# Node tiles of a graph transformer: distance between their starts, six slots where they are behind and ten elsewhere

## The chip, the cores and the metric

The kernel runs on one core of a Trainium2 chip. A core has a matrix engine (PE), a vector engine (DVE), a scalar engine (ACT), a general engine (POOL) that here only prepares gathers, and a queue engine (SP) that issues DMAs. The metric is the device time of one launch in microseconds (us); a lower time is better. The time before is the median of three runs, and beside it stands one execution that was recorded by the profiler.

## The reference

A graph of 6,250 nodes with 128 features and 200,000 edges, sorted by destination, goes through two layers of attention over edges and a feed-forward block; then comes a residual and a layer norm.

```python
for l in range(L):                                   # L = 2
    xn = _layernorm(x, ln1_g[l], ln1_b[l])
    deg = ...                                        # out-degree, normalised
    xp = xn + (xn @ Wpos[l] + bpos[l] + deg[:, None] * Wdeg[l][0] + bdeg[l])
    q, k, v = (xp @ Wq[l] + bq[l]), (xp @ Wk[l] + bk[l]), (xp @ Wv[l] + bv[l])   # 8 heads of 16
    att = jnp.einsum('ehd,ehd->eh', q[dst], k[src]) / scale       # one row per edge and self loop
    ex = jnp.exp(clip(att) - m[dst])
    alpha = ex / (s[dst] + 1e-16)
    aggr = segment_sum(v[src] * alpha, dst)
    x = x + (aggr @ Wo[l] + bo[l])
    h = gelu(_layernorm(x, ln2_g[l], ln2_b[l]) @ W1[l] + b1[l])
    x = x + (h @ W2[l] + b2[l])
return _layernorm(x0 + x)
```

## The kernel before

**The work.** Per layer there are edge units and node tiles. The edges lie in the order of their destination. 165 chunks of 1,024 edges each (`CA`) are gathered from the table of keys and values in memory: POOL issues eight indirect DMAs per chunk (`gather`, L1901). The edges of the last eight node tiles are instead handled as 56 blocks of seven tiles of edges, sorted by source: their rows are read in order and picked by matmuls, without POOL. Chunks and blocks are interleaved in a fixed list `UNITS` of 221 units. In layer 0 alone the eight sorts of these edges (`sort_tensor`, `sort_vector`, 23 steps each) run between the units; the first starts at slot 0, and seven more follow.

A unit goes through PE (queries spread over edges, L930 or L963), DVE (products with the keys L1595, sums per head L1604, clip L1607 and L1610), ACT (exponential L1193), DVE (messages L1619) and PE (sums by destination, L946 or L979), and DVE adds the sums to a ring of destination blocks (`add_sums`, L1645 for a chunk).

**The slots.** Every engine walks through the same numbered slots, in a Python loop at build time, and issues its part of each slot in that order; the engines wait for each other through semaphores only. Unit u takes slots 2u and 2u+1, and its sums are added in slot 2u+3. There are 444 slots with edge work (0 to 443). A slot can also hold steps of node tiles and, in layer 0, of sorts.

**The node tiles.** 49 tiles of 128 nodes follow the edges. A tile has the steps 0 to 32 in layer 0 and 0 to 26 in layer 1 (`STEPS`), one per slot from its start on. In short: step 0 loads its own rows, 2 to 4 make the self loop (L1307, L1779, L1783), 5 sums (PE L1025, L1028, L1032, L1033), 6 divides (DVE L1307, L1791), 8 to 12 the output projection and residual (PE L1043, L1047, DVE L1795), 13 and 14 a norm (ACT L1221 and L1223, DVE L1800), 16 to 20 the first feed-forward product and the gelu (PE L1050, L1054, ACT L1264 between the table loads L1260 and L1267), 22 and 23 the second (PE L1060, DVE L1803), 24 and 25 a norm (DVE L1813), 27 to 32 the next layer's queries, keys and values (PE L1064, L1067, DVE L1816, L1821) and their writing to memory. In layer 1 step 26 writes the result.

`TILES` is the order in which the tiles' edges become complete, `POS` a tile's place in it. The buffers of a tile (`work`, five of them, `WORK`) are taken in turn by place. The products of PE for node tiles, the sums of edge units and the products of the sorts take three banks of PSUM in turn (`node_bank`, `RING_BANKS`); `BANKED` names the steps of a tile that take one. Each use waits until the use three before it has been read (`bank_free`). At most two node tiles may take a bank in one slot (`used` in `node_starts`).

`node_starts` gives each tile its start: not before the slot after its last unit (`2 * last_unit(j) + 1`), and ten slots behind the tile before (`NODE_EVERY`), four for the last one (`NODE_LAST`). A tile is complete every 8 to 14 slots, now and then a second one comes close behind, and the starts slip back: place 8 starts 10 slots after it is ready, place 24 18 slots, place 47 44 slots. The last four starts are 459, 469, 479 and 483. Since the edge slots end with 443, layer 0 has 72 slots with node steps only (to 515) and layer 1 has 66 (to 509).

**What waits at the ends.** POOL runs up to four chunks ahead: chunk m reuses the buffer of chunk m-4 and waits for its messages (L1619). The first gather of layer 1, and the loads of queries, wait until the last tile of layer 0 has been written:

```python
def gather(e, l, c):
    m = l * CA + c
    if m >= RING_KV:
        e.wait_ge(msg_ready, chunk_unit(m - RING_KV) + 1)
...
for s in range(WORK):                                 # wait_tables, for l = 1
    e.wait_ge((kv_out, q_out)[of][s], 16 * layer_uses(s))
```

A second program for irregular graphs (`general`) is built into the kernel behind a branch; this input doesn't take it.

Of the kernel before, what the change touches and what calls it, by code (L numbers as in the profile page):

```python
# [27 lines left out]
NT = -(-N // P)  # L28
# [25 lines left out]
WORK = 5  # L54
# [79 lines left out]
def last_unit(j):  # L134

    return CHUNK_AT[min(CPT * (j + 1), CA - 1)] if j < JB else BLOCK_AT[(j - JB) * OB + OB - 1]
# [3 lines left out]
TILES = sorted(range(NT), key=lambda j: (last_unit(j), j))  # L140
POS = [TILES.index(j) for j in range(NT)]

NODE_EVERY = 10

NODE_LAST = 4
STEPS = (33, 27)

BANKED = {5: "sums", 8: "sums_t", 11: "out_proj", 16: "hidden_t", 19: "ff_in", 22: "ff_out",
          27: "next_t", 30: "qkv"}
# [5 lines left out]
def node_starts():  # L158

    starts, used = [], {}  # L160
    for j in TILES:
        behind = NODE_EVERY if len(starts) < NT - 1 else NODE_LAST
        start = max([2 * last_unit(j) + 1] + [s + behind for s in starts[-1:]])
        while any(used.get(start + k, 0) >= 2 for k in BANKED):
            start += 2
        starts.append(start)
        for k in BANKED:
            used[start + k] = used.get(start + k, 0) + 1
    return starts, used


NODE_STARTS, NODE_USES = node_starts()


def node_steps(l):

    slots = {}
    for j, start in zip(TILES, NODE_STARTS):
        for k in range(STEPS[l]):
            slots.setdefault(start + k, []).append((j, k))  # L180
    return [slots.get(u, []) for u in range(max(slots) + 1)]

GELU = 20
assert all((start + GELU) % 2 for start in NODE_STARTS)
SORT_STEPS = 3 * SA + 11


# [20 lines left out]
def at(slots, u):  # L210
    return slots[u] if u < len(slots) else []
# [37 lines left out]
def graph_transformer(nc, x, src, dst, Wq, bq, Wk, bk, Wv, bv, Wo, bo, Wpos, bpos, Wdeg, bdeg,  # L249
                      ln1_g, ln1_b, ln2_g, ln2_b, W1, b1, W2, b2, out):  # L250
    with ExitStack() as ctx:
# [922 lines left out]
        def scalar_fill(e, l, what, u, h):  # L1174
            n = unit(l, u)
            if what == "turn":


                one_hots(e, hotT[n % 2], n, "turn", h)
            elif what == "hot":  # L1180
                one_hots(e, hot[n % 2].rearrange("p t j -> p (t j)"), n, "hot", h)
            elif what == "source":
                one_hots(e, hot_source, n, "source", h)
            else:
                copy_rows(e, n, h)
# [48 lines left out]
        def node_scalar(e, l, j, k, held):  # L1234
# [19 lines left out]
            elif k == 17:  # L1254
                e.wait_ge(node_mm["hidden_t"], i)
                e.activation(col, ps("hidden_t")[:, 0:P], ACT.Identity, scale=cols[:, l, 4:5],
                             bias=cols[:, l, 5:6]).then_inc(hidden_ready, 1)
            elif k == GELU - 1:

                e.preload_act_table_set(GELU_TABLES)  # L1260
            elif k == GELU:
                e.wait_ge(node_mm["ff_in"], i)
# [12 lines left out]
        def scalar_edges(e):  # L1275
            for l in range(L):
# [8 lines left out]
                for slot in range(slots_of(l)):  # L1285
# [6 lines left out]
                    for fill_of in fills[2:]:  # L1292
                        scalar_fill(e, l, *fill_of)
                    for j, k in sorted(at(slots, slot), key=lambda of: (of[1] == GELU - 1) - (of[1] == GELU)):
                        node_scalar(e, l, j, k, True)
# [821 lines left out]
```

## Time and profile before

| | us |
|---|---|
| median of three runs | 3819.98 |
| lowest and highest | 3818.55, 3821.41 |
| the profiled execution | 3813.55 |
| its span, first to last instruction | 3811.8 |
| PE busy (matmuls) | 2966.6 |
| DVE busy | 2846.9 |
| POOL busy | 2572.7 |
| ACT busy | 1703.6 |

The profiled execution took 1.75 us more than its span and 6.4 us less than the median. Busy times are sums over stages that differ: a first stage without gathers, layer 0, a stretch without gathers, layer 1, and an end without gathers. So the share of an engine in the whole says little; the stages have to be read one by one. The names in the rows are those of the kernel's buffers; a row "A<-B" writes A from B.

### The profile page before, as it was taken

How to read it: one execution, taken by the hardware profiler on the slowest of the kernel's cores; microseconds unless marked ns; L12 is line 12 of the kernel's file. 1: busy time of each engine (PE TensorE's matmuls, PEld its weight loads, DVE VectorE, ACT ScalarE, POOL GpSimd, SP SyncE). 2: the span in 40 equal slices, each digit the busy share in tenths (PEclk: the TensorE clock that was granted, in tenths of full speed). 3: DMA queues.
4: the chain of work that ended last, by engine and by line, in shares of the span. 5: the costliest groups of instructions: out<-in, count | busy, mean ns of one | idle time of the engine just before them, and what ended most of it. 6: DMA issues, size and time to landing. Idle time of an engine off the chain costs nothing.

```text
span 3811.8 us, 71274 instructions
## 1 busy us (share of the span) xinstructions
PE 2966.6 (78%) x23989; PEld 2291.0 (60%) x23989; DVE 2846.9 (75%) x6650; ACT 1703.6 (45%) x4253; POOL 2572.7 (67%) x2665
## 2 busy tenths in 40 slices
PE   4874688888888888888776567778788787887876
PEld 3653566666666666666554356666566566666664
DVE  9886678788888788888774466777777777767774
ACT  1331235454545454545444135455454454544544
POOL 4007777777777777777752777777777777777770
PEclk6785689998989898999986678998898998889885
DMA  3015445555555455555542445555555555555540
GB/s 103 2 52 157 117 144 171 149 168 150 169 153 165 146 169 157 169 161 169 156 123 69 118 140 157 162 164 163 155 166 153 164 161 158 164 156 164 164 145 25
DMA packets 392799, 542.97 MB, mean 142 GB/s; under 512 B 77981, under 2 KB 304858, under 8 KB 392238
## 3 DMA queue, kind: packets, MB, share of 16 engines
q0 software_dynamic: 126720, 346.20, 31.1%
q1 hardware_dynamic: 258208, 184.95, 16.1%
q10 hardware_dynamic: 7506, 7.20, 0.6%
q8 instruction: 199, 3.26, 0.4%
q14 instruction: 166, 1.36, 0.1%
HBM read 512.93 MB, written 25.14 MB: 141 GB/s over the span
## 4 chain that ended last, share of the span: by engine, by line
POOL 44%; PE 19%; issue 17%; DVE 14%; ACT 3%; DMA 2%; SPq 0%; DVEq 0%; POOLq 0%; ACTq 0%
POOL kv_ring L1901 33%; POOL arena L1901 11%; PE psum L889 3%; PE psum L767 2%; DVE scratch L1595 2%; DVE att L1604 2%; DVE work L1307 2%; PE psum L1000 2%; PE psum L930 2%; PE psum L979 1%; PE psum L946 1%; PE psum L792 1%; DVE scratch L1619 1%; DVE arena L1645 1%; PE psum L1054 1%
## 5 line engine op out<-in xcount | busy, mean ns | idle before, releaser
L1901 POOL DMA_INDIRECT kv_ring<-kv_table,src_idx x1984 | 1897.9, 957 | 727.8 <-issue 599.7
L1160 ACT ACTIVATE scratch<-psum 128x512 f32<-128x512 f32 x1108 | 623.2, 570 | 540.7 <-PE psum L899 349.6
L1901 POOL DMA_INDIRECT arena<-kv_table,src_idx x656 | 624.0, 951 | 203.2 <-issue 196.5
L1595 DVE TENSOR_TENSOR scratch<-psum,kv_ring 128x512 f32<-128x512 f32 x496 | 318.7, 684 | 433.1 <-DMA kv_ring<-kv_table,src_idx 407.4
L930 PE MATMUL psum<-q_win,scratch 64*128 64x128 f32 x5280 | 446.3, 316 | 211.6 <-DVE scratch L1595 178.1
L930 PEld LDWEIGHTS psum<-q_win,scratch 64*128 64x128 f32 x5280 | 378.5, 216 | 330.4 <-issue 280.9
L1604 DVE TENSOR_REDUCE att<-scratch 128x64 f32<-128x1024 f32 (+1 forms) x442 | 519.5, 1175 | 0.1
L889 PE MATMUL psum<-arena 128*128 128x256 f32 x1568 | 458.7, 419 | 55.6 <-ACT arena L1171 53.8
L946 PE MATMUL psum<-scratch 128*64 128x136 f32 x5280 | 440.9, 317 | 23.6 <-DVE work L1791 8.3
L1193 ACT ACTIVATE psum<-att 128x64 f32<-128x64 f32 (+1 forms) x442 | 100.3, 227 | 682.5 <-DVE att L1610 675.5
L1171 ACT COPY arena<-psum 128x512 f32<-128x512 f32 x448 | 231.1, 532 | 385.4 <-PE psum L889 379.2
L946 PEld LDWEIGHTS psum<-scratch 128*64 128x64 f32 x5280 | 347.3, 155 | 65.6 <-issue 39.9
L889 PEld LDWEIGHTS psum<-arena 128*128 128x128 f32 x1568 | 284.0, 201 | 162.0 <-ACT arena L1171 107.8
L1595 DVE TENSOR_TENSOR scratch<-psum,arena 128x512 f32<-128x512 f32 (+1 forms) x388 | 235.9, 645 | 161.8 <-DMA arena<-kv_table,src_idx 127.2
L1619 DVE TENSOR_TENSOR scratch<-kv_ring,psum 128x1024 f32<-128x1024 f32 x248 | 299.7, 1208 | 4.2 <-ACT psum L1193 3.5
L1645 DVE SCALAR_TENSOR_TENSOR arena<-psum,in_block,arena 128x136 f32 x660 | 204.8, 351 | 56.2 <-PE psum L946 55.4
L979 PE MATMUL psum<-scratch 128*128 128x136 f32 x1568 | 237.7, 305 | 1.3 <-DVE arena L1713 1.3
L1619 DVE TENSOR_TENSOR scratch<-arena,psum 128x896 f32<-128x896 f32 (+1 forms) x194 | 219.4, 1131 | 6.3 <-ACT psum L1193 6.2
L979 PEld LDWEIGHTS psum<-scratch 128*128 128x128 f32 x1568 | 220.7, 211 | 3.7 <-issue 1.5
L899 PE MATMUL psum<-plan_mem,places 128*128 128x512 bf16 x330 | 138.5, 420 | 108.4 <-DMA plan_mem<-plan_table 52.7
L963 PEld LDWEIGHTS psum<-q_win,scratch 128*128 128x128 f32 x1568 | 193.3, 195 | 24.7 <-issue 18.3
L963 PE MATMUL psum<-q_win,scratch 128*128 128x128 f32 x1568 | 198.9, 280 | 11.4 <-DVE scratch L1595 11.1
(253 smaller groups left out, 4637.8 us busy)
## 6 DMA issues: line engine op xcount, KB each, us to landing
arena<-kv_table SPq DMA_DIRECT2D x112, 896.0 KB
kv_ring<-kv_table,src_idx POOLq DMA_INDIRECT x1984
q_win<-q_table SPq DMA_DIRECT2D x660, 32.0 KB
work<-kv_table SPq DMA_DIRECT2D x98, 128.0 KB
arena<-kv_table,src_idx POOLq DMA_INDIRECT x656
q_win<-q_table SPq DMA_DIRECT2D x112, 64.0 KB
work<-q_table SPq DMA_DIRECT2D x98, 64.0 KB
kv_table<-work SPq DMA_DIRECT2D x49, 128.0 KB, 2.4
```

What stands on the lines that cost most here:

```text
L889: mm = e.matmul(to[:, t % 2 * 2 * D:(t % 2 + 1) * 2 * D], hot_source[:, t * P:(t + 1) * P], source_rows[:, t, :], start=True, stop=True)
L930: m = e.matmul(q_edge[h][:, t * P:(t + 1) * P], hotT[n % 2][h * HALF:(h + 1) * HALF, t * P:(t + 1) * P], q_win[h * HALF:(h + 1) * HALF, n ...
L946: m = e.matmul(to[h * HALF:(h + 1) * HALF], by_edge[:, t * P + h * HALF:t * P + (h + 1) * HALF], msg[n % 2][:, h * T // 2 + t, :], start=t ...
L963: m = e.matmul(q_edge[f % 2][:, (t - ts[0]) * P:(t - ts[0] + 1) * P], hotT[n % 2][:, t * P:(t + 1) * P], q_win[:, n % 2, :], start=True, s ...
L979: m = e.matmul(edge_sum(l, u), hot[n % 2][:, t, :], msg[n % 2][:, t, :], start=t == 0, stop=t == last)
L1160: e.activation(to[:, at:at + width], apart[k % 2][:, 0:width], ACT.Relu, bias=1.0, scale=-1.0).then_inc(apart_read, 1)
L1171: e.copy(kv_block[:, ts[0]:ts[-1] + 1, :].rearrange("p t d -> p (t d)"), apart[k % 2][:, 0:len(ts) * 2 * D]).then_inc(apart_read, 1)
L1595: e.tensor_tensor(prod[:, ts[0] * P:(ts[-1] + 1) * P].rearrange("p (t d) -> p t d", d=D), q_edge[f % 2][:, 0:len(ts) * P].rearrange("p (t ...
L1604: e.tensor_reduce(raw_att.rearrange("p t h -> p (t h)"), prod[:, 0:ts * P].rearrange("p (g d) -> p g d", d=HD), AX_X, ALU.add).then_inc(sc ...
L1619: e.tensor_tensor(msg[n % 2][:, 0:ts, 0:D].rearrange("p t (h d) -> p t h d", d=HD), values.rearrange("p t (h d) -> p t h d", d=HD), ex[:, ...
L1645: e.scalar_tensor_tensor(out=row, in0=of_edges, scalar=in_block[:, k, i:i + 1], in1=row, op0=ALU.mult, op1=ALU.add).then_inc(acc_added, 1)
L1901: e.indirect_dma_start(kv[m % RING_KV][:, t, :], None, kv_table[l], bass.IndirectOffsetOnAxis(ap=src_idx[:, c * T + t:c * T + t + 1], axis ...
```

## The change

`node_starts` gets another rule. A tile still starts ten slots behind the one before, unless that would be more than four slots after it is ready (`NODE_BEHIND`); then it starts six behind (`NODE_SOON`), four for the last one. A start may not come before the tile five places earlier has gone through its 33 steps, since that one holds its buffer. `GELU` and the rule that a gelu stands in an odd slot move into the search, which now goes on by one slot instead of two.

```diff
+NODE_BEHIND = 4
+NODE_SOON = 6
 NODE_LAST = 4
 STEPS = (33, 27)
+
+GELU = 20
...
-    for j in TILES:
-        behind = NODE_EVERY if len(starts) < NT - 1 else NODE_LAST
-        start = max([2 * last_unit(j) + 1] + [s + behind for s in starts[-1:]])
-        while any(used.get(start + k, 0) >= 2 for k in BANKED):
-            start += 2
+    for i, j in enumerate(TILES):
+        ready = 2 * last_unit(j) + 1
+        before = starts[-1] if starts else ready - NODE_EVERY
+        start = max(ready, before + NODE_EVERY)
+        if start > ready + NODE_BEHIND:
+            start = max(ready, before + (NODE_SOON if i < NT - 1 else NODE_LAST))
+        if i >= WORK:
+
+            start = max(start, starts[i - WORK] + STEPS[0])
+
+        while (start + GELU) % 2 == 0 or any(used.get(start + k, 0) >= 2 for k in BANKED):
+            start += 1
```

Worked out by both rules (starts in slots; slots from 444 on hold no edge work):

| | before | after |
|---|---|---|
| place 8 (ready 79) | 89 | 83 |
| place 24 (ready 231) | 249 | 233 |
| place 36 (ready 333) | 369 | 339 |
| last five places | 449, 459, 469, 479, 483 | 413, 423, 433, 439, 443 |
| most that a start stands after ready | 44 | 8 |
| slots with node steps only, layer 0, layer 1 | 72, 66 | 32, 26 |
| slots with two node uses of a bank, layer 0 (with edge work) | 3 (0) | 51 (48) |

No two of the first 48 starts were other than ten apart. Now 34 gaps are ten, nine are six, three are eight and one is twelve. Steps worth 3.6 tiles in layer 0 and 3.7 in layer 1 move from behind slot 443 to before it. Three of the eight sorts still end in the slot where they did and five end one to three slots later, since a sort's product doesn't share a slot with two node uses. No instruction is added or removed in the program that this input runs; after the change all of it stands eight lines further down.

**DVE, end of layer 0.** After the last addition of edge sums (L1645, slot 443), before the change, in the queue of DVE:

```order
L1645 SCALAR_TENSOR_TENSOR arena<-psum,in_block,arena 128x136
L1307 SCALAR_TENSOR_TENSOR work<-work 128x1 x3
L1800 TENSOR_SCALAR work<-x_all,work 128x128
L1783 TENSOR_TENSOR work<-work 128x128
L1307 SCALAR_TENSOR_TENSOR work<-work 128x1 x3
L1813 TENSOR_SCALAR work<-x_all,work 128x128
L1307 TENSOR_SCALAR work<-psum 128x8
L1307 TENSOR_TENSOR work<-work,psum 128x8
L1307 RECIPROCAL work<-work 128x8
L1791 TENSOR_TENSOR work<-psum,work 128x128
L1816 SCALAR_TENSOR_TENSOR work<-wz_next,deg_z,b_next 128x384
L1821 TENSOR_TENSOR work<-psum,work 128x384
```

and after it, where L1653 is that addition and L1829 a tile's last step:

```order
L1653 SCALAR_TENSOR_TENSOR arena<-psum,in_block,arena 128x136
L1791 TENSOR_TENSOR work<-work 128x128
L1829 TENSOR_TENSOR work<-psum,work 128x384
L1803 TENSOR_TENSOR x_all<-x_all,psum 128x128
L1758 BN_STATS work<-x_all 128x6
L1760 BN_AGGR work<-work 128x2
L1315 TENSOR_SCALAR work<-psum 128x8
L1315 TENSOR_TENSOR work<-work,psum 128x8
L1315 RECIPROCAL work<-work 128x8
L1799 TENSOR_TENSOR work<-psum,work 128x128
```

Before, eight tiles have their last step (L1821) behind the last edge addition, 135 rows of the queue; after, five have it there (the first of them at once), 58 rows.

**PE, in the fifth sort (slots 190 and 191 of layer 0).** L1046 and L1047 are the output projection of one tile, L1000 a product of the sort, L979 the sums of a block. Before, with what each waits for:

```order
L1046 MATMUL psum<-rows,ones 128x128 [waits mean_col,acc_added]
L1047 MATMUL psum<-w_o,work 128x128
L1000 MATMUL psum<-arena 98x128 [waits sort_digit,sort_value,sort_tables,qkv_ready]
L1000 MATMUL psum<-arena 98x128 x9
L907 MATMUL psum<-places,plan_mem 128x128 [waits apart_read]
L907 MATMUL psum<-places,plan_mem 128x128 x3
L979 MATMUL psum<-scratch 128x136 [waits sort_picked,msg_ready]
```

After, where L1033 and L1036 are the sums (step 5) of the next tile, and L1008 the product of the sort:

```order
L1054 MATMUL psum<-rows,ones 128x128 [waits mean_col,acc_added]
L1055 MATMUL psum<-w_o,work 128x128
L1033 MATMUL psum<-work,ident 128x136 [waits acc_added,own_msg,qkv_ready]
L1036 MATMUL psum<-arena,ident 128x136
L915 MATMUL psum<-places,plan_mem 128x128 [waits apart_read]
L915 MATMUL psum<-places,plan_mem 128x128 x3
L987 MATMUL psum<-scratch 128x136 [waits sort_picked,msg_ready]
...
L1008 MATMUL psum<-arena 98x128 [waits sort_digit,sort_value,sort_tables,mean_ready]
```

Two node tiles use banks in slot 190 now, the sort's product has moved one slot back behind the block's sums, and it waits for the reader of the new tile's sums (`mean_ready`) instead of that of an older tile (`qkv_ready`).

## Rows read from the trace of the kernel before

**Rows 1.** The page's busy tenths of POOL in 40 slices of the span.

```profile
POOL 4007777777777777777752777777777777777770
```

**Rows 2.** Timeline of POOL: start us, us, engine, line, operation, idle before and releaser.

```profile
292.02 9.24 POOL L1901 DMA_INDIRECT kv_ring<-kv_table,src_idx  x1 [26.12 <-DMA kv_table<-scratch]
...
1979.80 0.95 POOL L1901 DMA_INDIRECT kv_ring<-kv_table,src_idx  x1 [0.30 <-issue]
2067.72 0.94 POOL L1901 DMA_INDIRECT kv_ring<-kv_table,src_idx  x1 [86.97 <-DMA kv_table<-work]
...
3717.82 0.94 POOL L1901 DMA_INDIRECT kv_ring<-kv_table,src_idx  x1 [0.30 <-issue]
```

**Rows 3.** Gathers by shape, layer 0 (292 to 1981 us): count, busy, mean ns, idle before.

```profile
L1901 POOL DMA_INDIRECT kv_ring<-kv_table,src_idx x992 | 959.1, 967 | 338.9 <-issue 299.3 <-DMA kv_table<-scratch 26.1 <-DVE scratch L1619 13.5
L1901 POOL DMA_INDIRECT arena<-kv_table,src_idx x328 | 313.6, 956 | 103.3 <-issue 97.2 <-DVE scratch L1619 6.1
```

**Rows 4.** The same of layer 1 (2067 to 3719 us).

```profile
L1901 POOL DMA_INDIRECT kv_ring<-kv_table,src_idx x992 | 938.8, 946 | 388.9 <-issue 300.4 <-DMA kv_table<-work 87.0 <-DVE scratch L1619 1.5
L1901 POOL DMA_INDIRECT arena<-kv_table,src_idx x328 | 310.4, 946 | 100.0 <-issue 99.3 <-DVE scratch L1619 0.6
```

**Rows 5.** Timeline of DVE, end of layer 0.

```profile
1993.28 0.63 DVE L1645 SCALAR_TENSOR_TENSOR arena<-psum,in_block,arena 128x136 f32 x2 [0.99 <-PE psum L946]
...
1995.95 0.17 DVE L1307 TENSOR_SCALAR work<-psum 128x8 f32<-128x8 f32 x1 [0.16 <-PE psum L1033]
...
2010.91 0.56 DVE L1821 TENSOR_TENSOR work<-psum,work 128x384 f32<-128x384 f32 x1 [3.03 <-PE psum L1067]
...
2021.21 0.56 DVE L1821 TENSOR_TENSOR work<-psum,work 128x384 f32<-128x384 f32 x1 [2.93 <-PE psum L1067]
...
2036.64 0.17 DVE L1307 TENSOR_SCALAR work<-psum 128x8 f32<-128x8 f32 x1
...
2064.49 0.56 DVE L1821 TENSOR_TENSOR work<-psum,work 128x384 f32<-128x384 f32 x1 [1.39 <-PE psum L1067]
```

**Rows 6.** Timeline of DVE, end of layer 1.

```profile
3730.59 0.63 DVE L1645 SCALAR_TENSOR_TENSOR arena<-psum,in_block,arena 128x136 f32 x2 [0.65 <-PE psum L946]
...
3733.84 0.17 DVE L1307 TENSOR_SCALAR work<-psum 128x8 f32<-128x8 f32 x1 [0.76 <-PE psum L1033]
...
3745.06 0.17 DVE L1307 TENSOR_SCALAR work<-psum 128x8 f32<-128x8 f32 x1 [0.76 <-PE psum L1033]
...
3778.51 0.17 DVE L1307 TENSOR_SCALAR work<-psum 128x8 f32<-128x8 f32 x1 [0.54 <-PE psum L1028]
...
3805.61 0.35 DVE L1813 TENSOR_SCALAR work<-x_all,work 128x128 f32<-128x128 f32 x1
```

**Rows 7.** Windows: stretch, its us, busy us and count of PE, PEld, DVE, ACT, POOL, PE clock, DMA share, GB/s.

```profile
1995.95:2036.64 40.69, 29.93 (x131) 20.72 (x131) 23.13 (x100) 25.43 (x60) 0.00 (x0) 0.71 0.13 39
3733.84:3778.51 44.67, 32.58 (x119) 24.82 (x119) 20.32 (x96) 24.11 (x56) 0.00 (x0) 0.50 0.11 29
292.00:1981.00 1689.00, 1384.75 (x11116) 1073.29 (x11117) 1341.83 (x3134) 778.09 (x1972) 1272.70 (x1320) 0.89 0.53 156
2067.00:3719.00 1652.00, 1271.00 (x10294) 981.11 (x10294) 1150.06 (x2708) 757.71 (x1914) 1249.14 (x1320) 0.86 0.53 156
```

**Rows 8.** Timeline of POOL in two of the sorts of layer 0.

```profile
548.41 0.94 POOL L1901 DMA_INDIRECT kv_ring<-kv_table,src_idx  x1 [5.14 <-DVE scratch L1619]
...
1314.17 0.94 POOL L1901 DMA_INDIRECT arena<-kv_table,src_idx  x1 [2.19 <-DVE scratch L1619]
...
1327.08 0.94 POOL L1901 DMA_INDIRECT kv_ring<-kv_table,src_idx  x1 [3.18 <-DVE scratch L1619]
```

**Rows 9.** Windows of layer 0: in a sort, and between two sorts.

```profile
1265.00:1330.00 65.00, 53.54 (x370) 41.38 (x368) 49.11 (x121) 26.18 (x70) 45.65 (x48) 0.84 0.47 140
1345.00:1465.00 120.00, 104.27 (x846) 81.93 (x845) 100.21 (x237) 59.53 (x152) 91.06 (x96) 0.93 0.54 160
```

More of the change, by code:

```diff
@@ L181, in node_steps @@
     return [slots.get(u, []) for u in range(max(slots) + 1)]
-GELU = 20
-assert all((start + GELU) % 2 for start in NODE_STARTS)
 SORT_STEPS = 3 * SA + 11
```

## The prediction, made before the changed kernel ran

> **What bounds the kernel now.** I read the page's slices first: POOL is busy at seven or eight tenths from slice 4 to the end, with a dip in the middle and nothing in the last slice [rows 1]. So there are two stages of gathers, and two stretches without them, one after each. POOL's timeline gives their edges [rows 2]: layer 0 gathers from 292.02 to 1980.8, then POOL is idle for 86.97 us until the last tile's keys and values are in memory, then layer 1 gathers from 2067.72 to 3718.8, and the last 93.0 us of the span (3811.8 - 3718.8) have no gather.
>
> Inside the gather stages the groups by shape tell whether POOL ever waits. In layer 1 it has 1320 gathers of 946 ns and 0.30 us of issue between them; the wait for a free buffer (DVE L1619) is 1.5 + 0.6 us in all [rows 4]. 1320 x 1.25 us = 1650 us, which is the whole stage (1651). Layer 1's middle is bound by POOL alone, with DVE busy 1150 of 1652 us and PE 1271 [rows 7]. Layer 0 is nearly so: 1688.8 us, 38 more. Of these the waits for DVE are 13.5 + 6.1 us [rows 3], and they stand in the sorts [rows 8]; the first gather takes 9.24 us [rows 2], 8.3 more than the others, and the rest comes from a mean of some 957 instead of 946 ns [rows 3].
>
> The stretches without gathers are bound by the node tiles. There a tile's last step on DVE (L1821) comes every 10.3 us in layer 0 (2010.91, 2021.21) [rows 5], and step 6 every 11.2 us in layer 1 (3733.84, 3745.06) [rows 6], while no engine is full: PE 29.9 and DVE 23.1 of 40.7 us [rows 7]. It is a chain through engines that walk the slots in order.
>
> **The change: what leaves the tails.** The slots with node steps only fall from 72 to 32 and from 66 to 26, so 40 slots in each layer. The last two starts have the same distance (479, 483 before; 439, 443 after). So the tail after should look like the tail before from slot 483 on, put directly behind the last edge addition. I take the time between two points 40 slots apart: step 6 of the tile that started at 439 (slot 445), and step 6 of the one that started at 479 (slot 485).
> Layer 0: 2036.64 - 1995.95 = 40.7 us [rows 5].
> Layer 1: 3778.51 - 3733.84 = 44.7 us [rows 6].
> Together 85.4 us.
>
> **What the remaining tails get.** The tiles before the last two are not at the old distances: relative to the last start they stood at -34, -24, -14, now at -30, -20, -10. In layer 0 that puts 3 + 4 + 4 = 11 more tile steps behind slot 443, 11/33 of a tile at 40.7/4 = 10.2 us, at most 3.4 us; in layer 1 4 + 4 = 8 of 27 at 11.2 us, at most 3.3 us. The bound below is 0, since the very last tile is a chain of its own that the others may fit beside. I take 2 us each, the middle, since steps of different tiles overlap only in part. -85.4 + 4.0 = -81.4.
>
> **What the gather stages get.** 3.6 and 3.7 tiles of steps move there. In layer 1 a tile keeps DVE busy for 20.3/4 = 5.1 us and PE for 32.6/4 = 8.1 us [rows 7]; 3.7 tiles are 19 us of DVE's 502 idle and 30 us of PE's 381. POOL waits 2.1 us in the stage today, so this cover is wide, and I cost it at 0. Were it gone, 3.7 x 11.2 = 41 us would come back.
> In layer 0 the cover is there between the sorts (POOL 91.06 busy of 120 us, which is its full rate of 96 gathers of 1.25) but not inside one: from 1265 to 1330 POOL made 48 gathers, which need 60 of the 65 us, and then waited 2.2 and 3.2 us for DVE [rows 8, 9]. In a sort each step added goes straight to POOL once its four buffers of lead are used up. In the seven later sorts, over the slots that each takes after the change, the two tables of starts put 69, 87, 81, 86, 77, 86, 78 node steps before, and 77, 91, 85, 97, 83, 97, 89 after: 55 more, of which 11 in the last sort, where POOL has no wait of its own. 44/33 = 1.33 tiles. The cheapest price is DVE's busy time, 23.1/4 = 5.8 us [rows 7], which gives 7.7 us; the dearest row is the full 10.2 us, which gives 13.6 us. The sorts of now also have slots in which two tiles take a bank, and products of the sort that wait for a reader in the same slot (mean_ready instead of qkv_ready); five sorts are stretched by one to three slots, which eases them. I take 10 us, nearer to the full price, since even in the sort DVE is busy 49 of 65 us and PE 54 [rows 9]: it is waits between engines that fill it. Below zero it can't go by much: all waits of POOL for DVE in layer 0 are 19.6 us with their 0.3 us of issue each [rows 3], so some 14 us is the most that another placing could win. The bound above: all 3.6 tiles at 10.2 us, 37 us.
>
> The starts now come 0 to 8 slots after a tile is ready instead of up to 44. The sums of step 5 need the edge addition of two slots after ready, three slots earlier at least. The first places had that distance before the change too (0, 2, 4 slots), so I cost it at nothing. SP's step 0 needs the write of the tile five places before, issued 32 slots after that one's start; the closest pair is now 44 slots apart, at more than 5 us a slot in the gather stages: covered. POOL's queue itself isn't changed, and DMAs are as many as before.
>
> **Sum.** -40.7 - 44.7 + 2 + 2 + 10 = -71.4 us. The span goes from 3811.8 to 3740.4 and the profiled execution from 3813.55 to 3742.2. That execution stood 6.4 us under the median of the runs, and I put the change on the median: 3819.98 - 71.4 = 3748.6 us, 1.9% less.
>
> **A rule that speaks against the change.** The gathers of layer 1 took 946 ns in the mean, in both groups, beside some 42 tiles' worth of node steps [rows 4]. The Trainium skill, "SBUF — State Buffer", section "Who interferes with whom", says that a DVE instruction in a two-port mode shuts POOL out of the port pair that the two share, for its whole duration, and that tensor_scalar can enter such a mode; L1800 and L1813 have that form. By that rule 7.3 moved tiles with two such steps of 0.35 us each would hold POOL up by some 5 us. The rows give no sign of it: both groups have the same mean, and POOL kept its full rate over the whole stage.
>
> **Rivals.**
> *Nothing is hidden in layer 0.* The moved steps of layer 0 cost their full 10.2 us wherever they stand, since the engines take their slots in order and waits between engines, not work, fill a slot. For it: busy shares of 75 to 82% in a sort that nevertheless held POOL up [rows 9]. Against it: between the sorts POOL ran at its full rate. It gives -85.4 + 4 + 37 = -44 us: 3776.
> *Sorts get lighter.* The slots by which five sorts are stretched take back POOL's waits; the extra steps then cost 0 and up to 14 us of waits go. -85.4 + 4 - 7 (half) = -88 us: 3732. Against it: there are more steps in each sort, not fewer.
> *The tail doesn't follow the slots.* The last tile waits for something else than its place in the order, such as the bank of a tile now 4 or 10 slots ahead; the tail then keeps one more tile per layer, 10.3 + 11.2 us: -50 us, 3770. For it: the only double uses before the change stood in this tail. Against it: the timeline of the tail has idle DVE in each period, up to 3.0 us before L1821 [rows 5].
> *Slower: the gathers themselves.* POOL is the bound for 2640 gathers in a row. If more node steps beside them lengthen each gather, the loss is 2640 times that. The gain of 71 us is gone at 27 ns each, and 30 ns gives 3828. For it: layer 0, with the sorts' steps on DVE, has means of 956 and 967 against 946 [rows 3, 4]. Against it: the 10 ns came with all of the sorts' vector work, and the moved steps are a tenth more of steps that cost nothing measurable in layer 1.
>
> **Chances.** Forecast, -60 to -84 us: 0.66. Nothing hidden in layer 0 or a part of it, -35 to -60: 0.14. Tail keeps a tile: 0.08. Lighter sorts: 0.08. Gathers lengthened: 0.02, and 0.02 for what I don't see. The range reaches from the lighter sorts to the first rival but its last few us: 3730 to 3774. A measurement of this kernel can tell about 0.2% (7.6 us) from no change. Faster by more than that: 0.96; within: 0.02; slower: 0.02.
>
> **What would show it.** In the profile after: POOL's idle time between the layers falls from 87.0 to about 48 us (87.0 - 38.7), and from the last gather to the end of the span from 93.0 to about 50. Layer 1's gathers still span 1651 us; if not, the cover was not there. Layer 0's span 1699 instead of 1689, with POOL's waits for L1619 at about 30 instead of 19.6 us; at 1725 the first rival is right. Means of 946 ns in layer 1 show that gathers aren't lengthened. If the tail between L1653 of slot 443 and the last L1829 is 33 us, the tail follows the slots; at 43 it kept a tile. The prediction is wrong if the time saved in both idle stretches isn't near 80 us, or if layer 0 gives back more than 37.

## The result, and the profile after

| | before | after |
|---|---|---|
| median of the runs, us | 3819.34 (4 runs) | 3759.07 (4 runs, 3757.21 to 3760.49) |
| profiled execution, us | 3813.55 | 3760.06 |
| its span, us | 3811.8 | 3758.3 |

The ratio of the two is 0.9841, with a 95% interval of 0.983 to 0.9853. So the change saves 1.6%, 60.3 us. (The kernel before has one run more here than in the section before the prediction, so its median is 3819.34 and not 3819.98.) The prediction was 3748.6 us (71.4 us saved), with a range of 3730 to 3774.

The lines of after that answer to [rows 2] are these, from POOL's timeline (start us, us, engine, line, operation, idle before and releaser). All lines of the kernel after stand eight further down, so L1909 is the gather and L1627 the messages of a unit.

```profile
2005.36 0.95 POOL L1909 DMA_INDIRECT kv_ring<-kv_table,src_idx  x1 [0.30 <-issue]
...
2056.18 0.94 POOL L1909 DMA_INDIRECT kv_ring<-kv_table,src_idx  x1 [49.88 <-DMA kv_table<-work]
...
3706.43 0.95 POOL L1909 DMA_INDIRECT kv_ring<-kv_table,src_idx  x1 [0.30 <-issue]
```

The first gather of after starts at 293.22. With it the span splits into the same five stretches as before, and the table says where the time went:

| stretch, us | before | after | difference | predicted |
|---|---|---|---|---|
| to the first gather | 292.0 | 293.2 | +1.2 | 0 |
| gathers of layer 0 | 1688.7 | 1713.1 | +24.4 | +10 |
| POOL idle between the layers | 87.0 | 49.9 | -37.1 | -38.7 |
| gathers of layer 1 | 1651.0 | 1651.2 | +0.2 | 0 |
| last gather to the end | 93.0 | 50.9 | -42.1 | -42.7 |
| sum | 3811.8 | 3758.3 | -53.5 | -71.4 |

(The sum of this one pair of executions is 7 us off the medians; more on that below.)

The gathers by shape (count, busy us, mean ns, idle before), layer 0 (293 to 2006 us) and then layer 1, answer to [rows 3] and [rows 4]:

```profile
L1909 POOL DMA_INDIRECT kv_ring<-kv_table,src_idx x992 | 958.6, 966 | 361.8 <-issue 297.8 <-DVE scratch L1627 37.9 <-DMA kv_table<-scratch 26.1
L1909 POOL DMA_INDIRECT arena<-kv_table,src_idx x328 | 316.4, 965 | 102.4 <-issue 99.0 <-DVE scratch L1627 3.4
...
L1909 POOL DMA_INDIRECT kv_ring<-kv_table,src_idx x992 | 939.0, 947 | 351.8 <-issue 300.7 <-DMA kv_table<-work 49.9 <-DVE scratch L1627 1.2
L1909 POOL DMA_INDIRECT arena<-kv_table,src_idx x328 | 310.3, 946 | 99.9 <-issue 98.4 <-DVE scratch L1627 1.5
```

Layer 1 is as before within a nanosecond. In layer 0 POOL waited 37.9 + 3.4 = 41.3 us for messages instead of 19.6. That is 22 of the 24 us; gathers into `arena` at 965 instead of 956 ns are 3 more.

The tails on DVE, of layer 0 (the last edge addition, the last L1829) and of layer 1 (the last edge addition, the last L1821), which answer to [rows 5] and [rows 6]:

```profile
2019.52 0.63 DVE L1653 SCALAR_TENSOR_TENSOR arena<-psum,in_block,arena 128x136 f32 x2 [1.56 <-PE psum L954]
...
2052.97 0.56 DVE L1829 TENSOR_TENSOR work<-psum,work 128x384 f32<-128x384 f32 x1 [1.69 <-PE psum L1075]
```

```profile
3719.66 0.63 DVE L1653 SCALAR_TENSOR_TENSOR arena<-psum,in_block,arena 128x136 f32 x2 [1.19 <-PE psum L954]
...
3752.36 0.35 DVE L1821 TENSOR_SCALAR work<-x_all,work 128x128 f32<-128x128 f32 x1
```

From the last edge addition to the end of the last tile's step it is 2053.53 - 2019.52 = 34.0 us in layer 0, where it was 71.8, and 33.1 us in layer 1, where it was 75.4.

### The profile page after: what moved, and what is told of

Its sections match the earlier page's. It is cut to its first block, busy times and chain, and to the rows that moved or that the text cites. A ratio compares the mean times of both kernels' runs of the same rounds, so it can differ in the third digit from the quotient of the medians.

```text
span 3758.3 us, 71004 instructions
## 1 busy us (share of the span) xinstructions
PE 2857.5 (76%) x23719; PEld 2260.2 (60%) x23989; DVE 2851.2 (76%) x6650; ACT 1699.5 (45%) x4253; POOL 2575.1 (69%) x2665
## 4 chain that ended last, share of the span: by engine, by line
POOL 42%; PE 21%; issue 16%; DVE 14%; ACT 4%; DMA 2%; DVEq 0%; SPq 0%; POOLq 0%; ACTq 0%
POOL kv_ring L1909 32%; POOL arena L1909 11%; PE psum L897 3%; PE psum L775 2%; PE psum L954 2%; DVE att L1612 2%; PE psum L987 2%; DVE scratch L1603 2%; PE psum L938 2%; DVE work L1315 1%; PE psum L1008 1%; PE psum L971 1%; PE psum L800 1%; DVE arena L1653 1%; DVE scratch L1627 1%
## 5 line engine op out<-in xcount | busy, mean ns | idle before, releaser
L1909 POOL DMA_INDIRECT kv_ring<-kv_table,src_idx x1984 | 1897.6, 956 | 713.6 <-issue 598.5
L1909 POOL DMA_INDIRECT arena<-kv_table,src_idx x656 | 626.7, 955 | 202.3 <-issue 197.4
L1627 DVE TENSOR_TENSOR scratch<-kv_ring,psum 128x1024 f32<-128x1024 f32 x248 | 299.8, 1209 | 7.6 <-ACT psum L1201 7.3
L1653 DVE SCALAR_TENSOR_TENSOR arena<-psum,in_block,arena 128x136 f32 x660 | 204.9, 352 | 91.6 <-PE psum L954 91.2
L1627 DVE TENSOR_TENSOR scratch<-arena,psum 128x896 f32<-128x896 f32 (+1 forms) x194 | 219.2, 1130 | 8.9 <-ACT psum L1201 8.8
L1168 ACT ACTIVATE arena<-psum 128x512 f32<-128x512 f32 x224 | 120.0, 536 | 124.2 <-PE psum L885 65.0
```

The source lines that it names most:

```text
L1168: e.activation(to[:, at:at + width], apart[k % 2][:, 0:width], ACT.Relu, bias=1.0, scale=-1.0).then_inc(apart_read, 1)
L1627: e.tensor_tensor(msg[n % 2][:, 0:ts, 0:D].rearrange("p t (h d) -> p t h d", d=HD), values.rearrange("p t (h d) -> p t h d", d=HD), ex[:, ...
L1653: e.scalar_tensor_tensor(out=row, in0=of_edges, scalar=in_block[:, k, i:i + 1], in1=row, op0=ALU.mult, op1=ALU.add).then_inc(acc_added, 1)
L1909: e.indirect_dma_start(kv[m % RING_KV][:, t, :], None, kv_table[l], bass.IndirectOffsetOnAxis(ap=src_idx[:, c * T + t:c * T + t + 1], axis ...
```

## The experiments

In all of them the first number is the length of layer 0's gather stage in the profiled execution, with POOL's waits for messages in it. The time of a whole execution says less: the stretch up to the first gather, which no run changes, took between 285.5 and 293.2 us in the profiles on the chips where POOL is the bound. Expectations give these waits net of the 0.3 us of issue that each contains: 14.0 us before the change, 36.4 after. The tables and the text here give them as the rows do (19.6 and 41.3).

### Only layer 1 takes the new starts

```diff
+NODE_STARTS, NODE_USES = old_starts()
+STARTS = [NODE_STARTS, node_starts()[0]]
...
-    for j, start in zip(TILES, NODE_STARTS):
+    for j, start in zip(TILES, STARTS[l]):
```

> Layer 0 keeps the old starts, layer 1 takes the new ones. If the two layers add up, POOL's gather stage of layer 0 stays at 1689 us, the idle time between the layers at 87 us, and only the end shrinks, from 93 to 51 us: 42 us less than before, about 3777 us. If the steps moved in layer 1 cost something in its gather stage after all, that stage is longer than 1651 us and the gain smaller.

Measured: 3775.0 us against 3812.42 of the kernel before on the same chip, ratio 0.9899 (0.9882 to 0.9915). The end after the last gather took 51.7 us, layer 1's gathers 1650.8. The moved steps of layer 1 are free and the whole gain of its tail is kept. Layer 0, which is the same program as before the change, took 1694.3 us, with 17.7 + 4.8 us of waits. So two executions of the same layer 0 differ by 5.6 us; differences below that are not read in what follows. From the two ratios, layer 0's part of the change is 0.9899 - 0.9841 = 0.0058, 22 us gained; by the two intervals this is known to some 8 us. Its idle stretch gave 37 to 39, so its gather stage lost some 16 us (8 to 24) over the runs and 24.4 in the one profiled.

### Every start of the kernel before four slots later

```diff
-        start = max([2 * last_unit(j) + 1] + [s + behind for s in starts[-1:]])
+        start = max([2 * last_unit(j) + 1 + 4] + [s + behind for s in starts[-1:]])
```

> The kernel before with every node start four slots later and nothing else: same distances, same number of steps in each sort to within two, sorts where they were. Theory work (each added step costs its price in a sort): layer 0's gather stage stays at 1689 us within 3. Theory placing (what counts is which node step falls beside which sort step): the stage moves by 5 to 20 us either way, though no step was added. Both tails are longer by some 4 us each.

Measured: 3823.93 against 3812.42 us, ratio 1.0032 (1.002 to 1.0044). Some of it is the longer tails (93.2 us idle between the layers, 96.2 at the end). Layer 0's stage took 1700.3 us. That is 11.6 more than in the profile of the kernel before, but only 6.0 more than the same layer 0 took in the run above, on this same chip. And of the 11.5 us between the medians the longer tails are 9.4. So the length of the stage alone proves little here. Gathers of layer 0 by shape:

```profile
L1901 POOL DMA_INDIRECT kv_ring<-kv_table,src_idx x992 | 955.8, 963 | 347.1 <-issue 298.4 <-DMA kv_table<-scratch 26.1 <-DVE scratch L1619 22.7
L1901 POOL DMA_INDIRECT arena<-kv_table,src_idx x328 | 315.5, 962 | 108.0 <-issue 98.7 <-DVE scratch L1619 9.3
```

The waits are 32.0 us instead of 19.6 (22.5 in the run above). By the two tables of starts, six of the seven later sorts have two to four node steps fewer beside them than before, and the last has two more. What no spread between executions explains is one wait in the third of these sorts, before the first gather of chunk 61 (counted from 0):

```profile
920.40 0.94 POOL L1901 DMA_INDIRECT kv_ring<-kv_table,src_idx  x1 [7.84 <-DVE scratch L1619]
```

The changed kernel waits 7.90 us before the same gather, and the kernel before doesn't wait there in either of its two profiled layers 0. A price per step can't give this. Which step of a tile falls beside which step of a sort counts too. Over the stage it is worth 6 to 12 us in these profiles, a quarter to a half of what the change lost in its own.

### The sorts on every second slot

Edit, on the changed kernel and on the kernel before:

```diff
             if k in SORT_BANKED:
                 slots.setdefault(u, []).append((s, -k))
+            if s and k < SORT_STEPS - 1:
+                u += 1
```

> The changed kernel with each of the seven later sorts on every second slot instead of every slot, so that it takes about 46 slots instead of 24. If the 24 us that layer 0 lost come only from the sorts being dense (by work or by placing), POOL's waits for DVE fall below 10 us and layer 0's gather stage comes down from 1713 to 1670 to 1685 us: 3715 to 3735 us in all. If the lost time comes from the moved node steps beside edge units as such, the stage stays near 1713 and the total near 3759.

> The kernel before with the sorts on every second slot. Its layer 0 stage should lose its 14 us of waits: from 1689 to about 1670 to 1675 us, total about 3800. Together with the run on the changed kernel it gives what the moved steps cost in layer 0 when no sort is dense: near 0 by both theories of the sorts (difference of the two runs 79 to 85 us), 24 us if the sorts have nothing to do with it (difference 60 us).

Measured: 3749.24 us with the new starts (ratio 0.9823, 0.9802 to 0.9844) and 3806.58 with the old ones (0.9981, 0.9971 to 0.9992). The stages are 1703.8 and 1686.2 us, with 34.4 and 13.9 us of waits (27.8 and 9.4 net of issue). Both expectations failed. Thinning the sorts takes 9 us from the new kernel, not 28 to 43, and its waits stay far above 10 us; it takes 2.5 us from the old one, which is less than two executions of one program differ by. The two stages are 17.6 us apart. The two medians are 57.3 us apart, near the 60 that the second expectation gave to "the sorts have nothing to do with it" and far from its 79 to 85.

So "a sort too dense" was the wrong picture. But the runs don't clear the sorts either: a sort on every second slot lasts 46 to 48 slots, and by the tables of starts 160 to 179 node steps stand beside each of the seven with the new starts, where it was 77 to 97. The steps were not taken away from the sorts; the sorts were spread over more of them. With the spread sorts POOL waited at other chunks, 48 to 50 and 119 to 124, near the ends of the longer sorts. That fits a sum of sort and node steps that uses up POOL's lead over a longer stretch, but no run tested this by itself.

### Catching up between the sorts

The rule is replaced by a list. The last four starts are those of the change, but gaps are 12 to 20 slots where a sort begins and six between sorts:

```diff
+STARTS = (15, 27, 39, 45, 51, 57, 69, 87, 93, 99, 105, 111, 123, 141, 147, 153, 159, 165, 183, 195, 201, 207, 213, 231, 243,
+          249, 255, 261, 273, 293, 299, 305, 311, 329, 339, 351, 357, 363, 369, 375, 387, 393, 399, 405, 411, 423, 433, 439, 443)
...
+    return list(STARTS), used
```

> The changed kernel with a fixed list of starts in place of the rule: the same last four starts (423, 433, 439, 443), so the same tails, but gaps of 12 to 20 slots where a sort runs and of six between the sorts. A sort now has 61 to 70 node steps beside it (73 to 81 before the change, 81 to 89 after), and 60 slots with edge work have two node uses of a bank instead of 48, nearly all outside sorts. Theory crowding (the moved steps cost time where they lie in a sort): POOL's waits in layer 0 fall from 36 to below 10 us, layer 0's stage to 1675 to 1685 us, and the whole is 28 to 38 us faster than the changed kernel. Theory double bank uses or steps beside edges as such: the stage stays at 1705 to 1720 us and the time is that of the changed kernel within 8 us.

Measured: 3731.77 us against 3816.94 of the kernel before, ratio 0.9786 (0.9764 to 0.9807). Gathers of layer 0 by shape:

```profile
L1901 POOL DMA_INDIRECT kv_ring<-kv_table,src_idx x992 | 958.8, 966 | 339.3 <-issue 299.6 <-DMA kv_table<-scratch 26.1 <-DVE scratch L1619 13.6
L1901 POOL DMA_INDIRECT arena<-kv_table,src_idx x328 | 315.8, 963 | 102.2 <-issue 98.4 <-DVE scratch L1619 3.8
```

POOL's waits are 17.4 us, about as before the change, and the stage is 1690.0 us, while the idle time between the layers is 48.84 us, as with the rule of the change.

The interval lies wholly below that of the change (0.983 to 0.9853). Against each one's kernel before it saves 82 us (0.0214 of 3817) instead of 60. This is the experiment that decides. Nearly as many steps moved, the tails are as short, there are more slots with two node uses of a bank (60 instead of 48), and the cost in layer 0 is gone. So neither the moved steps as such nor the double uses of banks outside sorts carry it: it is what stands beside the sorts.

It doesn't say what it is about the steps beside the sorts. Their number fell, but so did the slots of sorts with two node uses of a bank (from 20 to 2), and every step got another neighbour. The number alone is not it. Each of the seven sorts has fewer steps beside it here than in the kernel before, so by the number the waits had to fall below the 19.6 us of before, and they are 17.4; below 10 us and a stage of 1675 to 1685 us had been expected. By POOL's timeline all of them above 0.6 us stand in the last five sorts or just behind, 5.4 us (net of issue) at the last one, where the kernel before had none. And the run with the later starts had its 7.84 us in a sort without any double use. Which step meets which thus counts beside their number, and no run takes the two further apart.

### The gelu's table loads

ACT needs another table for the gelu and loads it and the old one again, 1.28 us each, while the edges' one-hot tiles queue behind on ACT. Edit on both kernels (the relu changes what is computed):

```diff
-                e.preload_act_table_set(GELU_TABLES)
...
-                    a = e.activation(..., ACT.Gelu, ...)
+                    a = e.activation(..., ACT.Relu, ...)
...
-                e.preload_act_table_set(TABLES)
```

> The changed kernel with a relu for the gelu and without the two table loads around it (the output isn't the reference's), on this chip. Theory ACT: layer 0's stage is at 1675 to 1685 us with waits below 10 us. Theory crowding on PE and DVE, with ACT beside it: waits fall by less than half.

> The same on the kernel before (output not the reference's). Theory ACT: waits near 0, the stage at 1672 to 1680 us, within 8 us of that of the run on the changed kernel. If the moved steps cost time by other engines, the two stages differ by 15 us or more, as those of the kernels with the gelu do.

Measured: 3745.43 us (0.9823, 0.9804 to 0.9843) and 3811.81 us (0.9993, 0.9982 to 1.0005). Gathers of layer 0 with the new starts:

```profile
L1908 POOL DMA_INDIRECT kv_ring<-kv_table,src_idx x992 | 960.2, 968 | 349.3 <-issue 299.0 <-DMA kv_table<-scratch 26.1 <-DVE scratch L1626 24.2
```

and with the old ones:

```profile
L1900 POOL DMA_INDIRECT kv_ring<-kv_table,src_idx x992 | 959.7, 967 | 337.2 <-issue 299.0 <-DMA kv_table<-scratch 25.9 <-DVE scratch L1618 12.3
```

The waits with the new starts are 24.2 + 5.2 = 29.4 us instead of 41.3, and the stage 1701.8 instead of 1713.1. With the old starts the stage stays (1688.9, where 1672 to 1680 was expected) and the waits are 12.3 + 2.6 = 14.9 us instead of 19.6, where none were expected. So the theory that ACT carries it all falls, since 29 us of waits remain with the new starts where under 10 were expected. But the table loads seem to have a share: the two stages are 12.9 us apart without them and 24.4 with them, between the 8 us that one theory allowed and the 15 of the other. With 5.6 us between two executions of one program, neither the size of that share nor, strictly, the share itself is shown.

### The same on another chip, and a fourth bank

> The changed kernel with the gelu replaced by a relu and without the two table loads around it (2.6 us of ACT per tile and layer); so the output isn't the reference's. Theory ACT: the moved tiles cost layer 0 time because a gelu with its table loads keeps ACT from the one-hots of the edges for 4 us, PE comes late with the sums and DVE with the messages. Then POOL's waits in layer 0 fall from 36 to below 10 us and the gather stage from 1713 to 1675 to 1685 us. Theory banks (three PSUM banks in turn for edges, sorts and up to two tiles a slot): the waits stay above 20 us. The tails shrink in any case.

> The same on the kernel before (output not the reference's for the same reason): what a gelu's table loads cost there. Theory ACT: waits fall from 14 to near 0 and the stage from 1689 to about 1672 us, so that the two kernels' stages differ by under 8 us. Theory banks: the difference between the two stays near 24 us.

> The changed kernel with four instead of three PSUM banks in turn (the exponentials of the scores go to SBUF, which frees a bank). Theory banks: POOL's waits in layer 0 fall from 36 to below 15 us, the stage to about 1690 us, total 3735 to 3742 us; DVE's waits for the edge sums fall from 65 to about 35 us. Theory ACT: stage and total within 5 us of the changed kernel.

> The kernel before with four banks. Theory banks: little to win, since no slot with edge work holds two node uses: stage 1680 to 1689 us. Against the run on the changed kernel: the difference of the two stages is under 8 us by theory banks and near 24 us by theory ACT.

The edit for the fourth bank, on each of the two kernels:

```diff
-RING_BANKS = 2, 6, 7
+RING_BANKS = 2, 3, 6, 7
...
-        ex = psum[:, 3, 0:T * H].rearrange("p (t h) -> p t h", t=T)
+        ex_rows = sb("ex_rows", [P, T * H])
+        ex = ex_rows[:].rearrange("p (t h) -> p t h", t=T)
```

These four ran on a chip on which the kernel before took 5710.55 us, and all four medians are read against that: 5637.48 and 5713.14 us without the table loads (0.9883 and 1.0006), 5511.12 and 5531.96 us with four banks (0.9678 and 0.9698). There POOL was not the bound. Its waits, from the profile of the kernel before without table loads (us in total, times, longest):

```profile
POOL kv_ring L1900 <- DVE scratch L1618: 1483.2, 179, 13.6
```

and a piece of PE's timeline of the same run, a weight load before which PE stood still with nothing in the profile to wait for:

```profile
1028.41 0.10 PEld L899 LDWEIGHTS psum<-plan_mem,places 128*128 128x128 bf16 x1 [17.34 <-issue]
```

Layer 1's gathers took 2530 us there instead of 1651. The expectations were written for a kernel bound by POOL, so they don't apply to these runs, and why that chip was slower is open. Three things can be read. The idle stretches shrank with the new starts there too: 107.6 to 67.4 us between the layers and 114.5 to 71.9 at the end without table loads, 108.6 to 73.5 and 114.5 to 74.3 with four banks. And in both kernels with the exponentials in SBUF single gathers had become longer: 971 and 972 ns in the mean of layer 1 instead of 948. Even so both were 3% faster than the kernel before there, so on a chip where POOL waits for the others the edit wins; how much of that is the fourth bank and how much the exponentials in SBUF, no run tells.

So the fourth bank was tried once more on a chip where POOL is the bound:

> The changed kernel with four PSUM banks in turn and the exponentials of the scores in SBUF, on a chip where POOL is the bound. In the earlier run the gathers took 972 ns in layer 1 instead of 948. If that holds here, layer 1's stage is 1320 x 0.024 = 32 us longer (1683 us) and a gather can be lengthened by DVE instructions with two SBUF inputs. Theory banks: PE's sums come earlier, POOL's waits in layer 0 are below 10 us, and layer 0's stage is some 1690 to 1700 us. Theory crowding without banks: waits stay above 15 us, since only the slower gathers themselves give the other engines time, and the stage is 1710 to 1730 us. Total 3765 to 3800 us.

Measured: 3889.47 against 3817.97 us, ratio 1.0189 (1.016 to 1.0219), slower than the kernel before. Gathers of layer 1 by shape:

```profile
L1910 POOL DMA_INDIRECT kv_ring<-kv_table,src_idx x992 | 989.1, 997 | 350.6 <-issue 301.2 <-DMA kv_table<-work 48.5 <-DVE scratch L1628 0.9
L1910 POOL DMA_INDIRECT arena<-kv_table,src_idx x328 | 331.9, 1012 | 100.0 <-issue 99.7 <-DVE scratch L1628 0.3
```

A gather took 997 and 1012 ns instead of 947 and 946, and the stage 1723.1 instead of 1651.2 us: 72 us, over twice what was expected. The timelines of POOL and of DVE in one piece of layer 1 show which gathers; L1628 makes the messages, and in this kernel both of its inputs are in SBUF:

```profile
2311.15 1.66 POOL L1910 DMA_INDIRECT kv_ring<-kv_table,src_idx  x1 [0.30 <-issue]
...
2321.87 1.10 POOL L1910 DMA_INDIRECT kv_ring<-kv_table,src_idx  x1 [0.30 <-issue]
...
2325.78 1.74 POOL L1910 DMA_INDIRECT kv_ring<-kv_table,src_idx  x1 [0.30 <-issue]
```

```profile
2310.78 1.21 DVE L1628 TENSOR_TENSOR scratch<-kv_ring,ex_rows 128x1024 f32<-128x1024 f32 x1
...
2320.94 1.21 DVE L1628 TENSOR_TENSOR scratch<-arena,ex_rows 128x1024 f32<-128x1024 f32 x1
...
2325.49 1.21 DVE L1628 TENSOR_TENSOR scratch<-kv_ring,ex_rows 128x1024 f32<-128x1024 f32 x1
```

The three long gathers start 0.37, 0.93 and 0.29 us after such an instruction and end 0.82 us behind its end, all three. Counted over layer 1, 217 gathers start while an L1628 runs. They take 1.27 us in the mean and up to 2.02; 158 of them take more than 1.0 us, and each of these ends 0.81 to 0.83 us behind the end of the L1628. The other 1103 gathers take 0.95 us in the mean and at most 1.02. After the change, where the exponentials are in PSUM, 214 gathers of layer 1 start while an L1627 runs, and none of them takes more than 0.96 us. So it is the second input in SBUF and not the fourth bank that lengthens them. The mechanism of the prediction's slower rival exists, then, with another instruction than most of the moved steps. On banks the run tells nothing: POOL's stage of layer 0 took 1774.9 us, 62 more than after the change, so the other engines had more time for each chunk and POOL waited for none of them, whatever the fourth bank did. That part is left open.

## Why the prediction was right, point by point

- **POOL bounds the gather stages and the tiles bound the stretches between.** Right. Layer 1's stage stayed between 1650 and 1653 us in every run on such a chip, with the moved steps and without, but for the one with the exponentials in SBUF.
- **40 slots leave each tail: 40.7 and 44.7 us, 2 us each given back.** Right on the profile, -37.1 and -42.1 against -38.7 and -42.7, and the run with only layer 1 changed gave 41.3 for the second. The tail of layer 0 was 34.0 us for 33 predicted; it follows the slots and no tile was kept.
- **Layer 1's moved steps cost 0.** Right: +0.2 us, and the run with only layer 1 changed.
- **Layer 0's moved steps cost 10 us: 44 steps in six sorts at 5.8 to 10.2 us per tile.** This is the term that was mis-sized, at 24.4 us in the profile and about 16 (8 to 24) over the medians. Its rows bounded it by 7.7 and 13.6; the 24.4 lie outside, and only the wider range with the first rival in it held them. Its place was right, for with other steps beside the sorts the cost went away. Its price was not. Sort by sort, from POOL's timelines and net of issue, the waits went from 4.9, 1.7, 1.4, 0.9, 4.8, 0.3 and 0 to 6.7, 6.8, 8.5, 2.9, 4.1, 2.4 and 5.0 us, while the steps added were 8, 4, 4, 11, 6, 11, 11. The two with the fewest steps added, the second and third, lost most (5.1 and 7.1 us). The last one, whose 11 steps the prediction left out because POOL had no wait of its own there, brought 5.0 of the 22.4. These are the longest wait in the third sort before, and after:

```profile
946.84 0.94 POOL L1901 DMA_INDIRECT arena<-kv_table,src_idx  x1 [1.68 <-DVE scratch L1619]
```

```profile
937.58 0.94 POOL L1909 DMA_INDIRECT kv_ring<-kv_table,src_idx  x1 [7.90 <-DVE scratch L1627]
```

  The full latency of a tile in the tail, 10.2 us, was taken as the dearest price. It is no upper bound inside a sort, where a step of a tile waits for sort and edge work that stands before it on three engines: 22.4 us of waits for 55/33 tiles are 13 us per tile, and shifting steps without adding any made POOL wait 9 to 12 us longer. The prediction had noticed that no engine is full in a sort and that waits fill it, and then took its two prices from a tail all the same, from the busy time there and from the pace of the tiles.
- **DVE waits for PE.** Not in the prediction. In layer 0 DVE's wait for the sums of chunks (L1653, formerly L1645) is the largest of its waits after the change; it was 34.4 us in 25 before:

```profile
DVE arena L1653 <- PE psum L954: 64.6, 42, 4.7
```

  With the table loads of ACT gone it is 46.7 us. PE's sums need the one-hots that ACT makes, and a gelu can delay these. If the two runs without table loads are taken at their word, this is between a third (of the waits, 14.5 instead of 21.7 us apart) and a half (of the stages, 12.9 instead of 24.4) of the loss. But this wait of DVE is also 50.2 us in the catch-up run, where the loss is gone, so a longer wait here need not reach POOL.
- **Spread of the measured numbers.** The profiled execution before the change stood 5.8 us below the median of the four runs (6.4 below that of the three that the prediction had), the one after 1.0 above. That is why the profile's -53.5 and the medians' -60.3 differ. The total came out within the stated range, but with some luck: 60.3 is at the very edge of the forecast's own band of 60 to 84, and the profile's 53.5 lies in the band that the prediction gave to "nothing hidden in layer 0 or a part of it". The two tails were worked out; that the sum is as near as 11 us is not a merit of the 10 us for layer 0.
- **Rivals.** "Nothing is hidden in layer 0" (+37 us) was nearer to the profiled stage (+24.4) than the forecast (+10), though not to the 16 us over the runs; the catch-up run rules it out, since there the moved steps cost nothing. "Lighter sorts" did not come: the sorts whose ends moved back got more waits, not fewer. The gathers of layer 1 were not lengthened (947 and 946 ns). In layer 0 some gathers are longer, before the change and after it, and they start beside DVE instructions whose inputs are all in SBUF: steps of the sorts, as the prediction guessed, but also one step of a tile that layer 1 doesn't have, L1816 (L1824 after). 15 gathers started while it ran before, with a mean of 1.16 us, and 22 after, with 1.14; together that is 1 us more.
- **Slips that change nothing.** The closest starts five places apart are 40 slots apart after the change, not 44, and a slot in layer 0's gather stage takes about 3.8 us (1688.7 us for some 440 slots), not more than 5; the write of the tile five places before still has 8 slots. And the steps moved in layer 0 are 123, or 3.7 tiles, not 3.6.

What stays open is how the 16 to 24 us divide between ACT's table loads, bank waits of a sort's products and plain order. It is shown only that they belong to what stands beside the sorts, and that order alone can make the longest of the waits.

## What to carry to other kernels

When an in-order schedule has a tail that only dependent steps fill, count slots in it and read the time of a slot from the trace: moving 40 slots under a saturated stage gave 37 to 42 us for 39 to 43 predicted, twice. Before filling a stage with the moved steps, find where its bound engine already waits, and keep them out of just these places; here nearly the same number of steps cost 24 us in the profile by a simple rule, and 1.3 us, less than two executions differ by, with a list that leaves gaps of 12 to 20 slots at the sorts. In such a place don't price a step by busy time: shift all steps by a few slots once and see how much that alone moves.

## What the runs showed of the hardware

A gather that POOL prepares takes 0.95 us. With a DVE tensor_tensor of 1.21 us running as it starts, both operands in SBUF, it takes up to 2.02 us, 1.27 in the mean, and the long ones end 0.82 us behind the end of that instruction. With the second operand in PSUM no gather of layer 1 that starts beside it takes more than 0.96 us. Over a stage of 1320 gathers beside 221 such instructions this was 72 us. The Trainium skill, "SBUF — State Buffer", section "Who interferes with whom", says that a DVE instruction with two SBUF inputs contends with a POOL instruction that reads SBUF; the trace agrees, with an indirect gather as that reader. The same section's rule on two-port modes was weighed in the prediction for L1800 and L1813. It shows next to nothing on these gathers: in layer 1 of the changed kernel 25 of them start while one of these two (L1808 and L1821 there) runs, and they take 0.951 us in the mean and at most 1.02.
